# Causal mask of the transposed scores: an accumulating identity matmul instead of a select on GpSimd

## What is computed

```python
q, k, v = split(x @ W_qkv.T)                       # each (B, 16, T, 16)
scores = einsum('bhqd,bhkd->bhqk', q, k) / sqrt(16)
scores = where(tril(ones(T, T)), scores, -inf)     # causal
attn = softmax(scores) @ v
x = layernorm(x + attn @ W_proj.T)
h = silu(x @ wg.T) * (x @ wu.T)                    # 768 wide, weights int / 127
x = layernorm(x + h @ wd.T)
```

## Time and profile before, and how to read it

| | before |
|---|---|
| three runs, us | 1554.58 median, 1554.26 to 1557.93 |
| profiled execution: span, first to last instruction, us | 1558.1 |
| instructions | 34187 |
| transposed scores (L1109), first and last start, us | 236.4 and 1195.4 |
| selects (L589), first and last start, us | 241.8 and 1196.1 |
| scores for the maxima (L1092), first and last start, us | 194.5 and 1153.8 |

### The profile page before, as it was taken

The page is one execution under the profiler, slowest core; times in us unless marked ns, Lnnn a source line. Parts: engine busy times, 40 slices in busy tenths (PEclk is TensorE's granted clock), DMA queues, the critical chain, the costliest instruction groups (busy, mean ns, idle before and its releaser), DMA issues.

```text
span 1558.1 us, 34187 instructions
## 1 busy us (share of the span) xinstructions
PE 1467.7 (94%) x9300; PEld 689.1 (44%) x9300; DVE 1208.7 (78%) x3122; ACT 940.5 (60%) x2055; POOL 353.7 (23%) x436
## 2 busy tenths in 40 slices
PE   8999969999998998998998998999898999999997
PEld 5665523333333333333333333333333666666664
DVE  4555577897897987987997987998762777887776
ACT  3545415776776775776776776777576444444443
POOL 5000001211211221221121121122121443444434
PEclk9999967999998999999999999999899999999999
DMA  7777993575475466457447547546401022212211
GB/s 246 229 238 229 232 138 42 72 86 67 62 90 73 56 83 85 57 74 90 61 66 91 67 57 92 71 61 110 65 13 38 28 81 81 69 52 81 81 55 41
DMA packets 173313, 140.58 MB, mean 90 GB/s; under 512 B 80208, under 2 KB 148304, under 8 KB 173136
## 3 DMA queue, kind: packets, MB, share of 16 engines
q1 hardware_dynamic: 173136, 138.46, 48.7%
HBM read 87.29 MB, written 50.33 MB: 88 GB/s over the span
## 4 chain that ended last, share of the span: by engine, by line
PE 83%; issue 6%; DVE 6%; DMA 3%; ACT 2%; SPq 0%; DVEq 0%; POOL 0%; POOLq 0%; ACTq 0%
PE ps L1180 18%; PE ps L1109 15%; PE ps L1092 14%; PE ps L1238 11%; PE ps L1055 7%; PE ps L1253 4%; PE ps L1151 4%; PE ps L1062 4%; DVE ps L841 3%; PE ps L1199 3%; DMA q_stack<-max_rows 1%; DVE row_max L841 1%; PE ps L1223 1%; PE ps L1044 1%; ACT x_hi_rows L738 1%
## 5 line engine op out<-in xcount | busy, mean ns | idle before, releaser
L841 DVE CUSTOM_DVE_ANT_0 ps<-ps,causal 128x1024 f32<-128x1024 f32 (+7 forms) x1024 | 746.1, 790 | 129.1 <-PE ps L1092 125.1
L700 ACT ACTIVATE probs<-ps 128x512 f32<-128x512 f32 (+3 forms) x1536 | 653.7, 495 | 274.4 <-PE ps L1109 265.6
L1109 PE MATMUL ps<-q_stack,k_stack 99*128 99x512 bf16 (+3 forms) x1536 | 402.7, 334 | 39.2 <-issue 19.5
L1092 PE MATMUL ps<-k_stack,q_stack 96*128 96x512 bf16 (+3 forms) x1536 | 361.8, 338 | 13.4 <-DVE row_max L841 5.9
L589 POOL TENSOR_SCALAR_AFFINE_SELECT probs<-probs 128x512 f32<-128x512 f32 x256 | 162.5, 635 | 806.8 <-ACT probs L700 806.8
L1180 PE MATMUL ps<-probs,v_ones 128*32 128x512 f32 (+3 forms) x3072 | 335.3, 509 | 0.5 <-POOL probs L589 0.5
L1109 PEld LDWEIGHTS ps<-q_stack,k_stack 99*128 99x128 bf16 x1536 | 132.8, 98 | 266.5 <-ACT probs L700 143.5
L1092 PEld LDWEIGHTS ps<-k_stack,q_stack 96*128 96x128 bf16 x1536 | 135.1, 99 | 187.5 <-DVE row_max L841 51.4
L619 POOL TENSOR_TENSOR h_lo<-h_sb,h_hi 128x512 f16<-128x512 f32 x96 | 119.3, 1248 | 197.9 <-ACT h_hi L757 197.9
L841 DVE DVE_READ_ACCUMULATOR2_ANT row_max<- 128x1 f32 x1024 | 145.9, 142 | 0.0
L749 ACT ACTIVATE silu<-ps 128x512 f32<-128x512 f32 x96 | 57.3, 597 | 127.5 <-PE ps L1238 127.5
(11 more groups left out here) (89 smaller groups left out, 1272.8 us busy)
## 6 DMA issues: line engine op xcount, KB each, us to landing
qk_parts<-parts SPq DMA_DIRECT2D x64, 384.0 KB, 2.8
q_stack<-qk_parts SPq DMA_DIRECT2D x192, 128.0 KB, 6.9
k_stack<-qk_parts SPq DMA_DIRECT2D x192, 128.0 KB, 7.3
x_sb<-in_L_attn_x SPq DMA_DIRECT2D x32, 512.0 KB, 4.5
v_rows<-v_sb SPq DMA_DIRECT2D x16, 512.0 KB, 3.2
v_flat<-v_rows SPq DMA_DIRECT2D x32, 256.0 KB, 10.8
attn_rows<-attn_sb SPq DMA_DIRECT2D x64, 128.0 KB, 2.1
v_sb<-attn_rows SPq DMA_DIRECT2D x16, 512.0 KB, 5.5
```

Of the source, the lines that this page charges most:

```text
L700: act.activation(probs[s % RING][:, j, 0:w], ps[:, 4 + n % 3, 0:w], ACT.Exp, scale=SOFT_SCALE).then_inc(exp_done, 1)
L841: last = dve.tensor_tensor_reduce(scores, scores, causal[:, T - w:T], 1.0, LOWEST, ALU.add, ALU.max, row_max[:, j * QT + qt:j * QT + qt + 1])
L1092: last = pe.matmul(ps[:, 2 * pair + c0 // CH, c0 % CH:c0 % CH + w], q_stack[g][0:ROWS, j, tile_cols(qt)], k_stack[g][0:ROWS, j, k0:k0 + w] ...
L1109: pe.matmul(ps[:, 4 + n % 3, 0:w * P], k_stack[g][0:ROWS_M, j, tile_cols(kt)], q_stack[g][0:ROWS_M, j, q0:q0 + w * P], start=True, stop=Tr ...
```

## The change

A constant `earlier` (bf16, 128 x 128) holds 0 where the key is not later than the query and -3.0e38 elsewhere. For a diagonal slot, TensorE adds it to the first 128 columns of the transposed scores by a second matmul into the same bank, identity times `earlier`; the exponential makes zeros of it. GpSimd's selects, their semaphore and their waits are gone; the product with v waits for the exponential in all slots. In the planner the select's time goes and a diagonal score is 54 longer; so the order of the steps comes out another way.

```diff
     COLS, EXP, ROW_MAX, PV, TURN = 54, (50, 107), (68, 134), (110, 214), 428
-    MASK, COPY, COPY_ROWS, NORMALISE, SPLIT = 594, 478, 158, 650, 950
+    COPY, COPY_ROWS, NORMALISE, SPLIT = 478, 158, 650, 950
...
                 order.append(("st", s, j))
-                pe += max(w * COLS, 90)
+                pe += max(w * COLS, 90) + (COLS if s % ns in diagonal else 0)
...
                     ready_at = act + ACT_PE
-                    if s % ns in diagonal:
-                        pool = max(pool, act + ACT_POOL) + MASK
-                        ready_at = pool + POOL_PE
...
+            pool.memset(earlier[:], 0.0).then_inc(consts_ready, 1)
...
+            pool.affine_select(out=earlier[:], in_=earlier[:], compare_op=ALU.is_ge, fill=LOWEST,
+                               base=0, pattern=[[1, P]], channel_multiplier=-1).then_inc(consts_ready, 1)
...
-            def mask(s, uses):
-
-                pool.wait_ge(exp_done, uses + 3)
-                pool.sem_inc(pool_passed, 1)
-                tile = probs[s % RING][:, :, 0:P]
-                pool.affine_select(out=tile, in_=tile, compare_op=ALU.is_ge, fill=0.0, base=0,
-                                   pattern=[[0, HG], [1, P]], channel_multiplier=-1).then_inc(masked, 1)
...
-                pe.matmul(ps[:, 4 + n % 3, 0:w * P], k_stack[g][0:ROWS_M, j, tile_cols(kt)],
-                          q_stack[g][0:ROWS_M, j, q0:q0 + w * P], start=True, stop=True).then_inc(st_ready, 1)
+                last = pe.matmul(ps[:, 4 + n % 3, 0:w * P], k_stack[g][0:ROWS_M, j, tile_cols(kt)],
+                                 q_stack[g][0:ROWS_M, j, q0:q0 + w * P], start=True, stop=s not in diagonal)
+                if s in diagonal:
+                    last = pe.matmul(ps[:, 4 + n % 3, 0:P], ident_bf[:], earlier[:], start=False, stop=True)
+                last.then_inc(st_ready, 1)
...
-                        if s in diagonal:
-                            pe.wait_ge(masked, at(b, g, ND, diagonal.index(s) + 1))
-                        else:
-                            pe.wait_ge(exp_done, bank_use(b, g, b_last, HG * s + HG - 1) + 1 + 3)
+                        pe.wait_ge(exp_done, bank_use(b, g, b_last, HG * s + HG - 1) + 1 + 3)
```

More of the change, by code:

```diff
@@ L53, in attention_steps @@
     COLS, EXP, ROW_MAX, PV, TURN = 54, (50, 107), (68, 134), (110, 214), 428
-    MASK, COPY, COPY_ROWS, NORMALISE, SPLIT = 594, 478, 158, 650, 950
-    PE_ACT, PE_DVE, ACT_PE, DVE_PE, ACT_POOL, POOL_PE = 240, 330, 150, 230, 230, 180
+    COPY, COPY_ROWS, NORMALISE, SPLIT = 478, 158, 650, 950
+    PE_ACT, PE_DVE, ACT_PE, DVE_PE = 240, 330, 150, 230
     ROWS_MOVED = 2700
@@ L59, in attention_steps @@
     whole = hg * sum(w for _, _, w in slots)
-    pe = act = dve = pool = o_free = 0
+    pe = act = dve = o_free = 0
     st_free, s_free = [0, 0, 0], [0, 0]
@@ L168, in block_kernel @@
     NM = HG * QT
-    ND = len(diagonal)
     NR = NE + 1
@@ L209, in block_kernel @@
         causal = sb("causal", [P, T], F32)
+        earlier = sb("earlier", [P, P], BF16)
         minus_half = sb("minus_half", [P, TILES], F32)
@@ L313, in block_kernel @@
         exp_done = sem("exp_done")
-        masked = sem("masked")
         pv_done = sem("pv_done")
@@ L548, in _ @@
             pool.memset(causal[:], 0.0).then_inc(consts_ready, 1)
+            pool.memset(earlier[:], 0.0).then_inc(consts_ready, 1)
             pool.memset(minus_half[:], -0.5)
-            pool.wait_ge(consts_ready, 3)
+            pool.wait_ge(consts_ready, 4)
+            pool.affine_select(out=earlier[:], in_=earlier[:], compare_op=ALU.is_ge, fill=LOWEST,
+                               base=0, pattern=[[1, P]], channel_multiplier=-1).then_inc(consts_ready, 1)
             pool.affine_select(out=causal[:, T - P:T], in_=causal[:, T - P:T], compare_op=ALU.is_ge, fill=LOWEST,
@@ L555, in _ @@
             pool.tensor_copy(ident_f16[:], ident[:]).then_inc(consts_ready, 1)
-            pool.wait_ge(consts_ready, 6)
+            pool.wait_ge(consts_ready, 8)
             for k, (name, n_, b_) in enumerate((("gate", wgate_n, wgate_b), ("up", wup_n, wup_b),
@@ L582, in _ @@
             expand_v(0, 0)
-            def mask(s, uses):
-                pool.wait_ge(exp_done, uses + 3)
-                pool.sem_inc(pool_passed, 1)
-                tile = probs[s % RING][:, :, 0:P]
-                pool.affine_select(out=tile, in_=tile, compare_op=ALU.is_ge, fill=0.0, base=0,
-                                   pattern=[[0, HG], [1, P]], channel_multiplier=-1).then_inc(masked, 1)
-            for s in range(AHEAD):
-                mask(s, bank_use(0, 0, False, HG * s + HG - 1) + 1)
-            def group_b(b, g, b_last):
-                last_group = b_last and g == NG - 1
-                for d, s in enumerate(s for s in range(AHEAD, NS if last_group else NS + AHEAD) if s % NS in diagonal):
-                    if d == 1 and not last_group:
-                        pool.wait_ge(pv_done, at(b, g, NS, RING))
-                        expand_v(b + 1 if g == NG - 1 else b, (g + 1) % NG)
-                    mask(s, bank_use(b, g, b_last, HG * s + HG - 1) + 1)
-                    if last_group and s == HQ - 1:
-                        inverse_deviation(0, ln1_step, 0)
+            def group_b(b, g, b_last):
+                if b_last and g == NG - 1:
+                    inverse_deviation(0, ln1_step, 0)
+                else:
+                    pool.wait_ge(pv_done, at(b, g, NS, RING))
+                    expand_v(b + 1 if g == NG - 1 else b, (g + 1) % NG)
             with pool.Fori(0, B - 1) as b:
@@ L830, in _ @@
                 dve.sem_inc(attn_stored[half], 16)
-            dve.wait_ge(consts_ready, 6)
+            dve.wait_ge(consts_ready, 8)
             def row_maxima(use, pair, u):
@@ L1078, in _ @@
             pe.wait_ge(preset, 6)
+            pe.wait_ge(consts_ready, 8)
             pe.sem_inc(pv_done, RING)
@@ L1121, in _ @@
                         pe.wait_ge(w_cast, casts[name])
-                        pe.wait_ge(consts_ready, 5)
+                        pe.wait_ge(consts_ready, 8)
                     if u >= 4:
```

## The result

| | before | after |
|---|---|---|
| median of 4 runs, us | 1555.62 | 1634.22 |
| lowest to highest, us | 1554.26 to 1557.93 | 1627.34 to 1635.5 |
| ratio, 95% interval | | 1.0502 [1.0476, 1.0527] |
| span of the profiled execution, us | 1558.1 | 1632.2 |

The change makes the kernel 5.0% slower, 78.6 us. The forecast was 60 us more, 1614.6 us. The measured time lies inside the whole range (1582 to 1642), but 4 us above the forecast's own part of it (1598 to 1630), where rival B stood.

The account below looks back on a forecast made before the run. TensorE was taken to set the end. Masks 57.3 us, less 12.8 at slot 9, plus 13.8 at the group's end and 3.4 for the clock, less about 2: +60 on 1554.6 gives 1614.6 us; range 1582 to 1642.

Parts of the forecast that it names:

- rival B: Group-end wait 0.95 us, slot 9's 0.40 us stays or reappears: 77 us, 90 with another wait; chance 0.17.
- What bounds the kernel: TensorE sets the end: busy 28.09 of a group's 28.40 us, waiting about 1.05 us.
- What is removed: 256 GpSimd selects, 162.5 us of its time, worth 0.5 us on the path, left out of the sum.
- What is added: 1024 mask matmuls of 128 columns on TensorE at 0.056 us each: 57.3 us, 1.8 us per group.
- Rival C: Loads of the identity not hidden: a mask's step 0.098 us, 100 us in all, 1655 us; chance 0.05.
- What is moved: The planner's new step order: 12.8 us less at slot 9, 13.8 us more at the group's end.
- Two places matter: Slot 9's 0.40 us wait goes; the group-end wait before the output's second turn becomes 0.8 to 0.95 us.
- rival F: Loop returns cost TensorE 3.28 us each; if that grew with the body, some 1 us x 6, within the range.
- The clock's term: About 0.06 of the attention runs at 1.2 GHz, where a mask costs double: 3.4 us more.
- A: Masks fall into TensorE's 34 us of waits, no new group-end wait: 23 us more, 1578 us, up to 1597; chance 0.2.
- D: GpSimd's select is the real pacemaker; without it up to 52 us of waits go, 1544 us; chance 0.03.
- E: The change does nothing measurable: masks dropped or costing 0.005 us each; chance 0.01.

Follow-up runs that it names:

- the second set: Changed kernel with the mask matmul added twice, each with -1.0e38 in place of -3.0e38: 1690.6 us, 1.0882 of the kernel before.
- the kernels with their own orders: Loop steps as a fixed list found by search, in place of the planner's: kernel before 1527.8 us, changed kernel 1593.7 us.
- selects, own order: Kernel before, selects kept, with its loop's steps as a fixed list in place of the planner's: 1527.8 us, 0.9829 of the kernel before.
- The written-out kernels: Loop over 7 sequences written out, no returns: kernel before 1520.3 us, changed kernel 1577.1, kernel before with a searched step list 1492.3.

## Why the prediction was right, and where it was off

The bound engine, the price of a mask and both waits that were named came out as forecast. Two terms were missing from the sum, the waits at slot 8 and the longer returns, and the time came to lie outside the forecast's own 1598 to 1630 us; that it is in the range is owed to the part of rival B that the range took in. A shorter first interval of stage B (7.2 us, below) helped, by luck.

**What bounds the kernel:** right. TensorE's chain share rose to 86%. My count of the waits, 1.05 us per group, was low: from every matmul's start it is 1.50 us.

**What is removed:** right, zero in both orders: a ratio of 0.9985 [0.9965, 1.0006] in the old one, the same group in the new one.

**What is added:** the step of 0.056 us was right; the work of a group rose by 1.79 us, the 1.8 forecast, and the second set and the kernels with their own orders come to 0.048 and 0.050 us each on the clock, with some waits filled or changes of mode saved. By the Trainium skill ("TensorE: Matmul & The Clock Gate", Back-to-back issue gap), 81 ns each, an estimate is 2.6 us per group; no run comes near it. (The 1638 us that the prediction gives for that rule are 1554.6 + 83 alone; put into its sum in place of the 57.3, the 83 make 1640.) Rival C is refuted: the load of the identity is hidden.

**What is moved:** the first failed step is "Two places matter". The wait at slot 9 went (-0.40 us, as forecast), and the wait at the group's end grew from 0.43 to 0.97 us (+0.54, forecast +0.43, the wait just above the 0.8 to 0.95 given). Both hold. What I missed is slot 8, where the new order puts four 512-wide scores in a row: 0.33 us of waits in place of 0.09, 8 us in all. I had read the new order at the places where the old one waited, and not at the places where the new one has more tiles in a row than banks.

**The loop, rival F:** the place was right, the mechanism was not, and its size was left out of the sum. "Some 1 us x 6" measured 8.4 - 6.1 = 2.3 us x 6 = 14 us, the largest miss. The step that failed is "if that time grew with the body": the first gap did not grow at all (3.2 us on average in both kernels). About half of the growth, 1.2 us per return, comes up to the second stop, which the masks ahead of the loop had moved 16 instructions nearer to the return; the other half comes behind it, where the lower clock lasts longer. The six returns cost 37 us before and 51 us after; I had the row of the first gap and priced the growth of it, and had not looked at the microseconds behind it, where the second one stands.

**Sum.** In the profile, the 31 intervals between turns of the maxima grew from 937.4 to 1010.7 us, by 73.3: 24 plain ones by 52.7 us (2.2 each, 1.79 of work and most of the rest waits), the six with a return by 27.8, and the first, where stage B begins, was 7.2 us shorter. Over the kernels run that first interval lies between 33 and 41 us, with and without masks, and I can't say why; the sum had nothing for it, and without it the time would lie near the top of the range. The clock's term, 3.4 us, is part of the returns. The spans differ by 74.1 us, the medians by 78.6.

The rivals: A (the waits swallow part) is true of the masks taken alone, 0.74 us of 1.79 in the new order and 0.43 in the old, but the order gave it back. B's figure, 77 us, is the nearest to the result, and its wait did come up elsewhere; yet a good part of what it added was the loop's. D and E are refuted.

## What to carry to other kernels

Work taken off an idle engine is worth what the bound engine waited for it, and here that was nothing; work put on the bound engine costs its steps, less the waits that it happens to fill, which a better order would have filled anyway. When an edit makes a planner write another order, time the order by itself: here it cost 42 to 47 us, and a better one gained 27. In a loop with a long body, look at the microseconds behind each return, and at the queue that fetches instructions: little is done there between two fetches, what stands ahead of the loop sets how much, and writing the loop out took the whole cost away.

## What the runs showed of the hardware

A return of the loop costs TensorE a gap of 2.8 to 3.7 us over all looped kernels, with or without masks, and in all but one (selects, own order) a second one that ends 3.4 to 5.4 us behind the return. Both end 1.4 to 2.0 us after a packet of the queue for TensorE's instructions has ended: at each return the trace has one packet that starts some 2.7 us ahead of it and one that starts 0.9 to 1.9 us behind it in the kernels before and after. That queue moves 1.34 MB in 82 packets before, 1.47 in 90 after and 1.61 in 98 with two masks: 16 KB each. The written-out kernels move fewer, 59 with selects and 67 with masks, and show no such gap. The Trainium skill ("Runtime: NRT & Kernel Launch", Instruction fetch mechanics) says that code comes in 16 KiB blocks fetched ahead in sequence, and that a taken branch out of the window has to wait for a fetch; the runs agree, and show besides that the block after the branch's target can be late too: 46, 30 or 14 instructions into the loop, as 0, 16 or 32 instructions of masks stand ahead of it. No run moved the loop's start and left all else as it was, so what that alone is worth was not timed; nor is it shown why the lower clock lasts 3.4 us at some returns and 10 at others.

A matmul of 16 columns with a load of 128 weights of its own takes 0.028 us up to the next one, one of 128 columns 0.058.
